# Feed-forward of a macaron block: routing weights copied to all partitions by DMA, gate weighted on GpSimd, down product in fp32

## The reference, cut to what matters

```
def ffn(x):                       # x is layer-normed, [4, 1024, 128]
    weights = routing_weights(x)  # [b, t, 8]; from x @ Wr, zone mask, top-2 fallback, normalized
    gate = einsum('btd,edi->beti', x, Wg)
    up   = einsum('btd,edi->beti', x, Wu)
    h = silu(gate) * up
    e_out = einsum('beti,eid->betd', h, Wd)
    return einsum('bte,betd->btd', weights, e_out)
x = x + 0.5 * ffn(layernorm(x))
x = x + attention(layernorm(x))
x = x + 0.5 * ffn(layernorm(x))
```

## Time and profile before

| | us |
|---|---|
| median of three runs | 1960.55 |
| profiled execution, its own time | 1962.79 |
| its span | 1960.7 |
| f1, first routing row stored to the last hw | 184.43 |
| f2, the same | 165.52 |
| VectorE busy in these two stretches | 170.63 and 134.89 |

### The profile page before, as it was taken

How to read it: one execution, slowest core, us unless ns; L and a number is a source line. 1 busy time by engine, 2 the same in 40 slices (tenths; PEclk the granted TensorE clock), 3 DMA queues, 4 the chain that set the end, 5 groups by cost and what they waited for, 6 DMA issues and landing times. The chain is left out here.

```text
span 1960.7 us, 50745 instructions
## 1 busy us (share of the span) xinstructions
PE 1689.8 (86%) x19952; PEld 1002.5 (51%) x19952; DVE 1789.6 (91%) x3488; ACT 1333.0 (68%) x1686; POOL 1261.7 (64%) x924
## 2 busy tenths in 40 slices
PE   4888659989998999999898899999999999986888
PEld 2445324555555555555555555555555555553555
DVE  6999888999999999999999999999999999967885
ACT  4555445777777777777777777777777777775554
POOL 2444334777777777777777777777677777752444
PEclk9999877999999999999999999999999999997999
DMA  5000021222222222222222222222222222100000
GB/s 157 2 1 1 1 73 45 57 57 56 60 67 60 63 72 74 57 57 57 57 57 56 57 57 65 65 58 75 71 62 57 57 56 57 41 3 1 12 12 23
DMA packets 102988, 98.78 MB, mean 50 GB/s; under 512 B 53600, under 2 KB 65888, under 8 KB 102496
## 3 DMA queue, kind: packets, MB, share of 16 engines
q1 hardware_dynamic: 99952, 94.68, 18.6%
q10 hardware_dynamic: 2800, 0.85, 0.2%
HBM read 7.67 MB, written 2.10 MB: 5 GB/s over the span
## 5 line engine op out<-in xcount | busy, mean ns | idle before, releaser
L1265 POOL TENSOR_TENSOR area<-area 128x624 f16<-128x624 f32 x512 | 745.3, 1460 | 360.2 <-ACT area L1224 226.7
L1145 DVE TENSOR_REDUCE area<-ps 128x1 f32<-128x512 f32 x1024 | 659.5, 680 | 9.6 <-PE ps L1040 7.4
L1221 ACT ACTIVATE area<-ps 128x1024 f32<-128x1024 f32 x512 | 524.7, 1025 | 198.0 <-PE ps L1069 164.5
L1224 ACT ACTIVATE area<-ps 128x1024 f16<-128x1024 f32 x512 | 522.4, 1020 | 0.0
L1086 PE MATMUL ps<-area 128*128 128x65 f16 x4096 | 469.5, 194 | 28.7 <-POOL area L1265 14.2
L1088 PE MATMUL ps<-area 128*128 128x64 f16 x4096 | 470.7, 196 | 0.0
L1090 PE MATMUL ps<-area 128*128 128x65 f16 x4096 | 467.5, 193 | 0.0
L1040 PE MATMUL ps<-area 128*128 128x512 f16 x1024 | 396.2, 387 | 57.4 <-DVE area L1145 43.1
L1086 PEld LDWEIGHTS ps<-area 128*128 128x128 f16 x4096 | 385.8, 97 | 114.2 <-DVE area L1171 36.6
L1171 DVE TENSOR_TENSOR area<-area 128x400 f16<-128x400 f32 x512 | 420.9, 822 | 23.8 <-ACT area L1224 12.0
L1088 PEld LDWEIGHTS ps<-area 128*128 128x128 f16 x4096 | 384.9, 98 | 67.7 <-issue 1.6
(11 more groups left out here) (165 smaller groups left out, 2464.9 us busy)
## 6 DMA issues: line engine op xcount, KB each, us to landing
area<-area SPq DMA_DIRECT2D x384, 128.0 KB, 2.4
area<-cv_all SPq DMA_DIRECT2D x32, 258.0 KB, 2.4
area<-wup SPq DMA_DIRECT2D x32, 256.0 KB, 3.3
area<-xt_hi SPq DMA_DIRECT2D x31, 256.0 KB, 2.5
area<-xt_lo SPq DMA_DIRECT2D x31, 256.0 KB, 2.8
xg<-in_x SPq DMA_DIRECT2D x4, 512.0 KB, 7.5
area<-in_wup SPq DMA_DIRECT2D x1, 2048.0 KB, 10.4
out_x<-xg SPq DMA_DIRECT2D x3, 512.0 KB, 3.2
```

The costliest lines, as they stand in the source:

```text
L1145: nc.vector.tensor_reduce(mx[:, hd, kh, qt:qt + 1], bank, AX.X, ALU.max).then_inc(s_mr, 1)
L1221: nc.scalar.activation(p32[:, s % 2, :], sc, ACT.Exp, scale=0.125).then_inc(s_e32, 1)
L1224: nc.scalar.activation(p_hi[:, s % 4, :], sc, ACT.Exp, scale=0.125).then_inc(s_e16, 1)
L1265: nc.gpsimd.tensor_tensor(p_lo[:, s % 4, DC:], p32[:, s % 2, DC:], p_hi[:, s % 4, DC:], ALU.subtract).then_inc(s_pp, 1)
```

## The change

For each unit one DMA on SyncE's queue copies the expert's row of routing weights (512 fp32 numbers, 2 KB, in one partition) to all 128 partitions of a buffer with four slots. ScalarE stores the transposed weights in fp32, one partition per expert (partitions 0 to 7). GpSimd multiplies silu(gate) by the copied weights (`gw`), VectorE multiplies that by up out of PSUM (`hw`), and the down product takes hw and the down weights in fp32: four matmuls of 128 columns. Line 784, the weight matmul, the two halves h_hi and h_lo and their ScalarE and GpSimd instructions go, as does the split of the down weights. The pieces of `route` and `norm` are spread anew, the next turn's weight rows are made two or three units earlier, and the pieces that split the attention's up weights are moved within f1. The output DMAs of f2 stand in the same list as the copies.

```
+            w_rows = carve(2 * 2 * 512).rearrange("p (t a n) -> p t a n", t=2, a=2)
+            w_all = carve(RING * 512).rearrange("p (s n) -> p s n", s=RING)      # RING = 4
 @block.sync
+                    def weights_to_all(i, t, k):
+                        if k % E == 0:
+                            sp.wait_ge(s_wt, 2 * t + (k // E + 1))
+                        if i >= RING:
+                            sp.wait_ge(s_gw, i - (RING - 1))
+                        row = w_rows[k % E:k % E + 1, t % 2, k // E, :]
+                        sp.dma_start(w_all[:, i % RING, :], row.unsqueeze(1).broadcast_to([1, P, 512])).then_inc(s_wa[i % RING], 16)
+                    def turn(t, last):
+                        for k in range(16):
+                            weights_to_all(t * 16 + k, t, k)
+                            if not first and t > 0 and k == 8:
+                                write_out(TB * (t - 1), TB * t, 2 * t + 1)
 @block.tensor
-                        nc.tensor.matmul(ps[:, 4 + k % 2, :], rows_sum[:, k % E:k % E + 1].broadcast_to([P, P]),
-                                         wt[:, k // E, :], start=True, stop=True).then_inc(s_wb, 1)
-                            nc.tensor.matmul(o, h_hi[:, b, cols], d_hi[:, e, :], ...)
-                            nc.tensor.matmul(o, h_hi[:, b, cols], d_lo[:, e, :], ...)
-                            last = nc.tensor.matmul(o, h_lo[:, b, cols], d_hi[:, e, :], ...)
+                            last = nc.tensor.matmul(ps[:, 6 + k // E, P * j:P * j + P], hw[:, b, P * j:P * j + P], wd32[:, e, :],
+                                                    start=(e == 0 and j == 0), stop=(e == E - 1), skip_group_check=True)
 @block.scalar
-                            nc.scalar.copy(h_hi[:, k % 2, :], hw[:, k % 2, :]).then_inc(s_hh, 1)
 @block.gpsimd
-                            nc.gpsimd.tensor_tensor(h_lo[:, k % 2, :], hw[:, k % 2, :], h_hi[:, k % 2, :],
-                                                    ALU.subtract).then_inc(s_hl, 1)
+                            pool.wait_ge(s_si, i + 1)
+                            pool.wait_ge(s_wa[i % RING], 16 * (i // RING + 1))
+                            if i >= 2:
+                                pool.wait_ge(s_hw, i - 1)
+                            nc.gpsimd.tensor_tensor(gw[:, k % 2, :], gate[:, k % 2, :], w_all[:, i % RING, :],
+                                                    ALU.mult).then_inc(s_gw, 1)
 @block.vector
-                                    (norm(v, t + 3, s_ch, s_rstd), {k: 1 for k in (2, 3, 4, 5, 6, 7, 14, 15)}, {k: 4 for k in range(2, 8)}),
-                                    (route(t + 1), {k: 1 for k in range(8, 13)}, {k: 5 for k in range(8, 13)})):
+                                    (norm(v, t + 3, s_ch, s_rstd), {}, {2: 5, 3: 5, 4: 5, 5: 5, 11: 4, 12: 4, 13: 4}),
+                                    (route(t + 1), {}, {k: 8 for k in range(7, 11)})):
-                            nc.vector.tensor_tensor(gu[:, b, :], gate[:, b, :], ps[:, 2 + b, :], ALU.mult).then_inc(s_gu, 1)
-                            nc.vector.tensor_tensor(hw[:, b, :], gu[:, b, :], ps[:, 4 + b, :], ALU.mult).then_inc(s_hw, 1)
+                            v.wait_ge(s_gw, i + 1)
+                            v.wait_ge(s_u, i + 1)
+                            v.wait_ge(s_dn, i + 1)
+                            nc.vector.tensor_tensor(hw[:, b, :], gw[:, b, :], ps[:, 2 + b, :], ALU.mult).then_inc(s_hw, 1)
```

More of the change, by code:

```diff
@@ L428, in _, with write_out @@
                 def _(sp):
+                    o_v = out.rearrange("(n p) d -> p n d", p=P)
+                    def weights_to_all(i, t, k):
[5 more added lines that the diff above has]
+                        sp.dma_start(w_all[:, i % RING, :], row.unsqueeze(1).broadcast_to([1, P, 512])).then_inc(s_wa[i % RING], 16)
+                    def write_out(n0, n1, added):
+                        sp.wait_ge(s_y, added)
+                        sp.dma_start(o_v[:, n0:n1, :], xs[:, n0:n1, :]).then_inc(s_out, 16)
+                    def turn(t, last):
[3 more added lines that the diff above has]
+                                write_out(TB * (t - 1), TB * t, 2 * t + 1)
                     if first:
                         load_sync(sp)
+                    turns(turn)
+                    if first:
                         sp.wait_ge(s_rope, 16)
                     else:
[L434 to L442, removed]
+                        write_out(TB * (B - 1), TB * (B - 1) + 4, 2 * B)
+                        write_out(TB * (B - 1) + 4, TB * B, 2 * B + 1)
                         sp.wait_ge(s_out, (B + 1) * 16)
@@ L476, in weight_rows @@
                         for j in range(4):
-                            last = nc.tensor.matmul(ps[0:2 * E, 6, P * j:P * j + P],
-                                                    whl[:, 4 * a + j].rearrange("p h e -> p (h e)"), ident16[:],
-                                                    start=(j == 0), stop=True, skip_group_check=True)
+                            last = nc.tensor.transpose(ps[0:E, 6, P * j:P * j + P], w[:, 4 * a + j, :], ident[:])
                         last.then_inc(s_wr, 1)
@@ L536, in turn @@
                                 transpose(t + 1, (k - 1) // 2)
[L537 to L540, removed]
+                            if not last and k in (11, 12):
+                                weight_rows(t + 1, k - 11)
                     pe.sem_inc(s_dn, 2)
                     if first:
-                        pe.wait_ge(s_id, 3)
+                        pe.wait_ge(s_id, 2)
                     transpose(0, 0)
@@ L595, in rows @@
                         act.wait_ge(s_wr, 2 * p + (a + 1))
-                        nc.scalar.copy(wt[0:2 * E, a, :], ps[0:2 * E, 6, :]).then_inc(s_wt, 1)
+                        nc.scalar.copy(w_rows[0:E, p % 2, a, :], ps[0:E, 6, :]).then_inc(s_wt, 1)
                     def silu(i, t, k):
                         act.wait_ge(s_g, i + 1)
-                        if not (t == 0 and k == 0):
-                            act.wait_ge(s_gu, i)
+                        if i >= 2:
+                            act.wait_ge(s_gw, i - 1)
                         nc.scalar.activation(gate[:, k % 2, :], ps[:, k % 2, :], ACT.Silu).then_inc(s_si, 1)
@@ L608, in turn @@
                                 silu(i + 1, *((t, k + 1) if k < 15 else (t + 1, 0)))
-                            act.wait_ge(s_hw, i + 1)
-                            act.wait_ge(s_dn, i + 1)
-                            nc.scalar.copy(h_hi[:, k % 2, :], hw[:, k % 2, :]).then_inc(s_hh, 1)
+                            if first and k == 9:
+                                up_high(act, t)
                             if not last:
@@ L687, in route @@
                                            nc.vector.tensor_scalar, nc.vector.tensor_reduce)
-                        w_all, fb_all = (ex[:, m].rearrange("p (t e) -> p t e", e=E) for m in range(2))
+                        zone, fb_all = (ex[:, m].rearrange("p (t e) -> p t e", e=E) for m in range(2))
                         idx = rev[:].unsqueeze(1).broadcast_to([P, TB, E])
```

94 lines of the change are left out of this document (31 added, 63 removed).

## The result

The changed kernel takes 2699.32 us (median of four runs, 2696.08 to 2702.32) for 1960.44 us of the kernel before: ratio 1.376, 95% interval 1.374 to 1.378. I had forecast 2913 us, a slowdown of 953 where 739 was measured; the direction, the place and the mechanism came as said, the size was 214 us too large. The stated range, 1928 to 3020 us, was wide enough to hold the case of hidden copies as well, so that 2699 lies in it says little; what carries the forecast is the mechanism, and the price of one copy.

A forecast was written before the change was run, and what follows sets the result against it. VectorE was taken to pace f1 and share f2 with TensorE before the change. Copies then bind: +464.5 (f1), +483.4 (f2), +4.8 (outputs) make +952.7 on 1962.8, 2915.5, or 2913 us against the median; range 1928 to 3020.

The forecast's parts named there:

- hidden copies: Rival, both feed-forwards: only the written side binds, the ring hides the copies, TensorE sets the pace; 1945 us, chance 0.24.
- What bounds: Both feed-forwards: copies at 10.08 us against units of 2.88 or 2.59 us bind, hiding all engines' work; chance 0.60.
- One sign: Both feed-forwards: if the forecast is right, every engine is busy under a third there.
- The copy's price: Each unit's 262 KB copy out of one partition at 26 GB/s: 10.08 us, 645.1 us per feed-forward.
- my own range: Whole kernel if copies bind: 2780 us (9 us a copy, neighbours overlapping a little) to 3060 us (11.2 us).
- f2: Second feed-forward: copies add 483.4 us, and three output DMAs between them in the queue add 4.8 us.
- Dear fp32: Rival, down product with copies hidden: 0.44 us per fp32 matmul, 3.25 us of TensorE a unit; 2033 us, chance 0.07.
- What goes: Removed VectorE products (42.3 us in f1), ScalarE roundings (38.9 us in f1) and 64 TensorE matmuls: hidden behind DMA, paying nothing.

The follow-up runs named there:

- wide reads: Changed kernel with each 256 KB copy reading 128 partitions of the rotary table instead of one row: 1936.69 us (0.9876).
- interleaved experts: Changed kernel with experts taken in the order 0 4 1 5 2 6 3 7, so neighbouring copies read different groups of four partitions: 2265.67 us (1.1554).

## Why the prediction was right, and where its size was off

- *What bounds.* That the copies would bind in both feed-forwards and nothing else would count held: DMA share 0.86 and 0.85, GpSimd waiting for the copy for some 8.4 us in each long step, attention the same (f1's last hw to f2's first stored row: 1564.3 us before, 1562.6 after). One sign failed: I had every engine under a third busy, and TensorE is busy for 247.8 of 536.3 us, 46%, at a granted clock of 0.67.
- *The copy's price is the mis-sized term,* in two parts. I took 26 GB/s, from 2 KB going into one partition, and 10.08 us a copy. That it lies near 27.2 is in part luck: the row is the mean of a window of 0.08 us, its halves show 39 and 13 GB/s (below), and it writes into one partition where the copies read out of one. (a) One way gives 27.2 GB/s, 9.63 us: 0.45 x 64 = 29 us less for each feed-forward. (b) I let copies follow strictly one another. Each time the group of four partitions changes, two overlap and the step before is 4.3 us on the mean for 9.63; that is at 16 of the 63 steps of f1, 16 x 5.3 = 85 us. Together 114 us for f1; predicted +464.5, measured +352.7 (the last hw ends at 576.96 for 224.25), 112 less; the long steps are 9.7 on the mean, so the 63 steps give 110, and the first row was stored 1.7 us earlier than before. I had named such an overlap in the lower end of my own range (9 us a copy) but sized it far too small: it is 8.33 on the mean, outside that range.

```profile
719.62:719.66 0.04, 0.04 (x2) 0.04 (x1) 0.04 (x1) 0.04 (x1) 0.04 (x1) 1.00 0.22 39
719.66:719.70 0.04, 0.04 (x2) 0.04 (x1) 0.04 (x1) 0.04 (x1) 0.04 (x1) 1.00 0.09 13
```

- *Why reading, not writing:* I had chosen this between 0.81 and 84 us by the nearest row, and said that the trace could not tell reads from writes. The wide reads settle it.
- *The Trainium skill's port rule* (SBUF — State Buffer, "Door 1: The DMA port swizzle": four neighbouring partitions on one port of about 27 GB/s) would have given 9.6 us, and the trace agrees to the second digit (9.63), groups of four included; the 199 for 324 GB/s that I called agreement with its half is 0.61. The kernel time by that rule, 2855 us, is 156 us too long for the same reason as mine, the overlaps. The same page's section "Can I just issue two DMAs to hit both halves?" has two concurrent DMAs, on tiles at partitions 0 and 64, at only 6% more than one. For copies of single rows out of partitions 0 to 7 the runs here disagree, 55 GB/s for 32 with interleaved experts, and the measurement decides.
- *f2.* Predicted +483.4 and +4.8 for the outputs. The last hw ends at 2692.53, the rows were stored at 2139.60: 552.9 us for 165.5, +387.4. From its first stored row (38.08) f1 takes 538.9 us, so f2 takes 14.0 more. All of it lies in the three turns that have output DMAs: the first turn, which has none, is 139.1 us long in both, and from there to the last gate f2 takes 399.8 us where f1 takes 385.8. Steps of 12 to 19 us stand there from unit 8 to 9, where the list has the output DMAs. I had 4.8 us for the three; 14.0 is some 4.7 for each, where I had 1.6. No run takes them out, so the cause rests on this comparison.
- *The hidden case* would have been 1936.69 us (wide reads) for my 1945: the fp32 matmuls at 0.89 us a unit (0.88 said), a turn of 42 to 44 us in f1 and 39.4 in f2 (42.6 and 39.6 in my sum). The make-up was another: TensorE's step is 2.19 us (2.35 said with the extras) and the halts are longer, ScalarE's wait for the weight rows among them (25.8 us in f1), which the sum did not have. Dear fp32 (2033 us) was wrong.
- *What goes pays nothing* while the copies bind: right, VectorE stands 424.3 us for GpSimd in f1. The fp32 product alone is 31 us faster than the kernel before.

## What to carry to other kernels

Before letting a DMA spread one row over all partitions, price the side that is read: bytes times 128 over the rate of one way (27 GB/s here), not over the rate of wide copies. The same row read out of HBM landed in 3.2 us, and the kernel took 1942 us, near the 1937 of wide reads; rows that must stay in SBUF are best read from alternating groups of four partitions and in fewer bytes. Where a change bundles a costly and a cheap part, run the cheap one alone: here it was the better kernel.

## What was not expected of the hardware

- Copies from different groups of partitions reach little more than twice one group's rate (27.2 GB/s) from one queue: 4.55 us each with rows in partitions 0, 4 ... 28 and eight slots, 4.8 with two groups; from two queues 3.9 us (66 GB/s for 59). At the start of a feed-forward even these are used nearly one after the other (8.5 us with two groups, 7.2 with eight).
- Reading one 2 KB row of HBM 128 times lands in 3.2 us; a row in SBUF read as often took 9.63 us of transfer alone.
- Without GpSimd's difference and ScalarE's rounding, the 502 VectorE instructions of f1 took 23 us less, some 20 of them in small instructions that read only SBUF (1191 to 219 ns in one line); the products out of PSUM stayed at 683 ns.
